# Half of the first layer's feed-forward, moved in 32 pieces into the first attention

## What is computed

```python
xn = _layernorm(x, axis=-1)
x = x + _L0_attn_ref(xn, Wq, Wk, Wv, Wo) + _L0_ffn_ref(xn, w_gate_up, w_down)
# _L0_attn_ref: 16 heads of 16, rotary embedding, causal softmax over 1024 tokens, output projection
# _L0_ffn_ref:
gate, up = jnp.split(jnp.einsum('bsh,oh->bso', xn, w_gate_up), 2, axis=-1)   # 1024 each
out = jnp.einsum('bsi,hi->bsh', jax.nn.silu(gate) * up, w_down)
```

## Time and profile before

| | us |
|---|---|
| three timed runs | 2784.49, 2780.20, 2782.88; median 2782.88 |
| profiled execution, its own time | 2753.76 |
| its span, first to last instruction | 2752.0 |
| Heads0, end (first matmul of Ffn at 448.13) | 448.1 |
| Ffn of layer 0, 448.1 to 617.1 | 169.0 |
| mean granted TensorE clock over the span | 0.979 |

### The profile page before, as it was taken

The page is one execution under the profiler, slowest core; times in us unless marked ns, Lnnn a source line. Parts: engine busy times, 40 slices in busy tenths (PEclk is TensorE's granted clock), DMA queues, the critical chain, the costliest instruction groups (busy, mean ns, idle before and its releaser), DMA issues.

```text
span 2752.0 us, 41999 instructions
## 1 busy us (share of the span) xinstructions
PE 2601.9 (95%) x16786; PEld 1644.6 (60%) x16786; DVE 1599.5 (58%) x3476; ACT 1064.0 (39%) x1954; POOL 926.3 (34%) x934
## 2 busy tenths in 40 slices
PE   7988988999999999999999998879999999979996
PEld 4445544664556565565665556646666666656896
DVE  6676672226575664756655232767778877754332
ACT  2534553114444534445445111533444444333222
POOL 3221210003232322322222001626666666654222
PEclk8999999999999999999999999989999999989998
DMA  6222211008000000000000200000000000036223
GB/s 191 63 62 63 62 47 62 0 4 148 1 1 1 1 1 1 1 1 1 1 16 1 106 0 31 1 13 17 17 15 16 15 15 17 14 130 190 62 72 134
DMA packets 57139, 109.54 MB, mean 40 GB/s; under 512 B 13793, under 2 KB 32481, under 8 KB 55793
## 3 DMA queue, kind: packets, MB, share of 16 engines
q1 hardware_dynamic: 53152, 96.47, 12.5%
q0 software_dynamic: 3792, 10.39, 1.0%
HBM read 71.16 MB, written 27.08 MB: 36 GB/s over the span
## 4 chain that ended last, share of the span: by engine, by line
PE 86%; DVE 8%; ACT 2%; issue 1%; DMA 1%; POOL 1%; SPq 1%; POOLq 0%; DVEq 0%; ACTq 0%
PE ps L1256 9%; PE ps L1238 8%; PE ps L1780 5%; PE ps L1247 5%; PE ps L1228 5%; PE ps L378 4%; PE ps L1265 4%; PE ps L360 4%; PE ps L365 4%; PE ps L1897 4%; PE ps L1826 4%; PE ps L2914 3%; PE ps L2938 3%; PE ps L697 2%; PE ps L721 2%; PE ps L737 2%
## 5 line engine op out<-in xcount | busy, mean ns | idle before, releaser
L1256 PE MATMUL ps<-back 128*128 128x512 f32 x576 | 292.0, 596 | 0.3 <-ACT back L1299 0.3
L1299 ACT ACTIVATE back<-ps 128x512 f32<-128x512 f32 x288 | 170.0, 597 | 266.3 <-PE ps L1247 264.7
L1294 ACT ACTIVATE back<-ps,front 128x128 f32<-128x128 f32 (+7 forms) x256 | 189.1, 739 | 71.6 <-DVE front L1345 69.5
L1388 POOL TENSOR_TENSOR back<-back 128x512 f32<-128x512 f32 x72 | 91.5, 1271 | 361.7 <-DVE back L1333 361.5
L1247 PEld LDWEIGHTS ps<-front,back 128*128 128x128 f32 x1152 | 140.8, 141 | 118.4 <-issue 95.0
L1398 POOL TENSOR_SCALAR back<-back,front 128x128 f32<-128x128 f32 (+5 forms) x192 | 143.1, 749 | 191.0 <-DVE front L1364 188.3
L809 ACT ACTIVATE back<-ps 128x1024 f32<-128x1024 f32 (+1 forms) x192 | 150.8, 811 | 127.9 <-PE ps L721 127.4
L1345 DVE TENSOR_REDUCE front<-ps 128x1 f32<-128x128 f32 (+7 forms) x256 | 194.0, 758 | 8.8
L1247 PE MATMUL ps<-front,back 128*128 128x128 f32 x1152 | 170.5, 273 | 3.3 <-DVE back L1370 3.3
L1338 DVE TENSOR_TENSOR ps<-ps,front 128x128 f32<-128x128 f32 x256 | 76.0, 297 | 166.1 <-PE ps L1238 166.1
L697 PE MATMUL ps<-rounded 128*128 128x512 f32 (+3 forms) x384 | 140.9, 410 | 12.6 <-DMA rounded<-kh 4.3
(11 more groups left out here) (320 smaller groups left out, 5562.8 us busy)
## 6 DMA issues: line engine op xcount, KB each, us to landing
whole<-l_w SPq DMA_DIRECT2D x32, 512.0 KB, 5.2
front<-back SPq DMA_DIRECT2D x128, 64.0 KB, 2.0
rounded<-qh SPq DMA_DIRECT2D x28, 256.0 KB
rounded<-kh SPq DMA_DIRECT2D x56, 128.0 KB
front<-xg SPq DMA_DIRECT2D x47, 129.0 KB
xg<-front SPq DMA_DIRECT2D x2, 3008.0 KB, 34.1
front<-l_win SPq DMA_DIRECT2D x1, 4640.0 KB, 17.7
front<-l_wgu SPq DMA_DIRECT2D x2, 2048.0 KB, 13.3
```

What stands on the lines that cost most here:

```text
L1256: e.matmul(PS[:, 7, :], self.V[:, j, G % 4 * 128:G % 4 * 128 + 128], self.turned(("turn", n, j)), start=(j == 0), stop=(j == qt)).then_inc ...
L1294: e.activation(self.P[n % 2][:, h, :nk], s[:, :nk], ACT.Exp, bias=st[:, 0, h:h + 1], scale=1.0, accum_out=st[:, 1, h:h + 1]).then_inc(A.se ...
L1299: e.activation(self.turned(step), self.bank(step), ACT.Copy).then_inc(A.sem, 1)
```

## The change

Of layer 0's feed-forward, tokens 0 to 1023 (8 groups t of 128 tokens) are computed within Heads0, the other 1024 stay in Ffn (`t0=2`).

- New steps `ff` 0 to 31 (four for each t): gate and up for 256 features and 128 tokens, 8 matmuls of 128 columns into one bank of the ring. ScalarE makes tanh(gate/2) into one buffer `th`; VectorE makes (th + 1) * gate, waits for itself, and makes that * 0.5 * up into one of four buffers `H`: silu(g) = g * (tanh(g/2) + 1) / 2.
- New steps `fd` 0 to 7: the down projection for 128 tokens, 8 matmuls of 256 columns, and one addition to x on VectorE.
- Places in time (`pieces`): two `ff` before the first unit's M transpose and two after it; then for each of units 1 to 14 one at three quarters of it and one just at the start of the next. `fd` 0 comes ahead of unit 1, `fd` 1 to 7 in the middle of units 3, 5, ..., 15.
- w_down is loaded in two halves after the first moves at the start, no longer at the end; `high` and `low` are half as long, so the two token halves of a projection share a buffer, and copies wait for the landing of the half before (`kept`, now one semaphore for each k, tt, x).
- Ffn runs tt = 2, 3 only; the norms of groups 0 and 1 are made behind ups 0 to 5 (`stats` and `rows` behind ups 0 and 3, `turn` behind 1 and 4, `out` behind 2 and 5). For t0 = 0 its order is as before.

The diff, cut to its core:

```diff
+        self.t0, self.ups, self.downs = t0, 8 * (4 - t0), 2 * (4 - t0)
...
-        for tt in range(5):
+        for tt in range(t0, 5):
             rest = [[("down", tt - 1, 0), ("down", tt - 1, 2), ("stats", tt - 1)], [("rows", tt - 1)],
-                    [("turn", tt - 1)], [("out", tt - 1)]] if tt else [[]] * 4
+                    [("turn", tt - 1)], [("out", tt - 1)]] if tt > t0 else [[]] * 4
             for f in range(8 if tt < 4 else 0):
                 self.order.add("up", tt, f)
+                if tt == t0 and f < 3 * t0:
+                    for kind in (("stats", "rows"), ("turn",), ("out",))[f % 3]:
+                        self.order.add(kind, f // 3)
...
-        self.low = [sb(WF0 + 4096 + 1024 * i, 1024) for i in range(2)]
+        self.low = [sb(WF0 + 4096 + 512 * i, 512) for i in range(2)]
+        self.Wd = [sb(WF0 + 5120, 4, 256), sb(WK0 + 17408, 4, 256)]
+        self.H = [sb(at, 256) for at in (EX0 + 512, EX0 + 768, WA0 + 12560, WF0 + 6144)]
+        self.th = sb(WK0 + 18944, 256)
...
-        self.high = [sbr(at + 16384 + 1024 * i, 1024) for i in range(2)]
+        self.high = [sbr(at + 16384 + 512 * i, 512) for i in range(2)]
...
+           "act": {"proj": 0.1, "v": -0.2, "s2": -0.15, "o": -0.05, "at": -0.2, "ff": -0.1},
...
-            elif step[0] in ("proj", "s1", "out", "ot"):
+            elif step[0] in ("proj", "s1", "out", "ot", "ff", "fd"):
...
+        if not pool:
+            for i, t in enumerate(self.pieces(begin, length)):
+                add(t, "ff", i)
+            if not act:
+                for i in range(8):
+                    add(begin[2 * i + 1] + (0.5 * length[2 * i + 1] if i else -0.25), "fd", i)
...
+    def pieces(self, begin, length):
+
+        at = [-0.07, -0.06, begin[0] - 0.04, begin[0] - 0.03]
+        for u in range(1, 15):
+            at += [begin[u] + 0.75 * length[u] + 0.14, begin[u + 1] + (0.12 if u in (7, 8) else 0.01)]
+        return at
...
+    def wait_kept(self, w, k, x, tt):
+
+        if tt > 0:
+            w.wait_ge(self.kept[k][0][x], 32)
+        elif k > 0:
+            w.wait_ge(self.kept[k - 1][1][x], 32)
...
+            elif kind == "ff":
+                t, f = step[1] // 4, 2 * (step[1] % 4)
+                w.wait_ge(self.ffn.arrived, self.ffn.total)
+                w.wait_ge(self.norm.out, t // 4 + 1)
+                o = self.take(w, step)
+                for side in range(2):
+                    for a in range(2):
+                        c = side * 1024 + (f + a) * 128
+                        at = side * 256 + a * 128
+                        for j in range(2):
+                            i = e.matmul(o[:, at:at + 128], self.Wgu[:, j, c:c + 128], XNT[:, j, t * 128:t * 128 + 128],
+                                         start=(j == 0), stop=(j == 1))
+                i.then_inc(P.sem, 1)
+            elif kind == "fd":
+                t = step[1]
+                w.wait_ge(self.wd_in, 32)
+                o = self.take(w, step)
+                w.wait_ge(self.results, self.dn["ff", 4 * t + 3])
+                for f in range(8):
+                    i = e.matmul(o[:, 0:256], self.H[f // 2][:, f % 2 * 128:f % 2 * 128 + 128],
+                                 self.Wd[f // 4][:, f % 4, :], start=(f == 0), stop=(f == 7))
+                i.then_inc(P.sem, 1)
...
-                e.activation(self.high[x][:, tt * 512:tt * 512 + 512], self.ra[x], ACT.Copy).then_inc(A.sem, 1)
+                self.wait_kept(w, k, x, tt)
+                e.activation(self.high[x], self.ra[x], ACT.Copy).then_inc(A.sem, 1)
...
+            elif kind == "ff":
+                w.wait_ge(self.products, self.pn[step])
+                if step[1] > 0:
+                    w.wait_ge(self.results, self.dn["ff", step[1] - 1])
+                e.activation(self.th, self.bank(step)[:, 0:256], ACT.Tanh, scale=0.5).then_inc(A.sem, 1)
...
+            elif kind == "ff":
+                n = step[1]
+                H = self.H[n % 4]
+                w.wait_ge(self.activations, self.an[step])
+                if n > 3:
+                    w.wait_ge(self.products, self.pn["fd", n // 4 - 1])
+                e.scalar_tensor_tensor(H, self.th, 1.0, self.bank(step)[:, 0:256], ALU.add,
+                                       ALU.mult).then_inc(self.half_done.sem, 1)
+                w.wait_ge(self.half_done, n + 1)
+                e.scalar_tensor_tensor(H, H, 0.5, self.bank(step)[:, 256:512], ALU.mult, ALU.mult).then_inc(D.sem, 1)
+            elif kind == "fd":
+                t = step[1]
+                w.wait_ge(self.products, self.pn[step])
+                before = ("out", 0, t // 2 * 2)
+                if self.dn[before] < self.dn[step]:
+                    w.wait_ge(D, self.dn[before])
+                e.tensor_tensor(X[:, t, :], X[:, t, :], self.bank(step)[:, 0:256], ALU.add).then_inc(D.sem, 1)
...
-                e.tensor_tensor(self.low[x][:, o], self.ra[x], self.high[x][:, o], ALU.subtract).then_inc(G.sem, 1)
+                self.wait_kept(w, k, x, tt)
+                e.tensor_tensor(self.low[x], self.ra[x], self.high[x], ALU.subtract).then_inc(G.sem, 1)
...
+        for i in range(2):
+            e.dma_start(self.Wd[i], self.net.ins["l0_wd"][:, 4 * i:4 * i + 4, :]).then_inc(self.wd_in.sem, 16)
...
-        w.wait_ge(self.results, self.dn["proj", 3, 1, 1, 0])
-        w.wait_ge(self.results, self.dn["proj", 3, 1, 1, 1])
-        e.dma_start(self.Wd, self.net.ins["l0_wd"]).then_inc(self.ffn.arrived.sem, 16)
...
-    f = Load(net, "w_ffn", [(Wgu, "l0_wgu")], 1)
-    h.plan(net, f, Norm(net, work=h.work, x=x), zeros)
+    f = Load(net, "w_ffn", [(Wgu, "l0_wgu")])
...
-    ffn = Ffn(net, Wgu, h.Wd, f, Norm(net, work=beside, inside=True, last=0))
+    ffn = Ffn(net, Wgu, [h.Wd[k // 4][:, k % 4, :] for k in range(8)], f, Norm(net, work=beside, inside=True, last=0), t0=2)
...
```

More of the change, by code:

```diff
@@ L907, in dve @@
                 w.wait_ge(self.products, self.pn[step])
+                for t in range(i, i + 2 if b == 0 else i):
+                    if self.dn["fd", t] < self.dn[step]:
+                        w.wait_ge(D, self.dn["fd", t])
                 e.tensor_tensor(x, x, self.bank(step).rearrange("p (a b) -> p a b", a=2), ALU.add).then_inc(D.sem, 1)
@@ L1191, in pe @@
         w.wait_ge(f.norm.out, 3)
-        w.wait_ge(f.x, 7)
+        w.wait_ge(f.x, f.downs - 1)
         for step in self.orders[0]:
@@ L3060, in stages @@
     q = Quantize(net)
-    ffn = Ffn(net, Wgu, Wd, f, Norm(net, work=beside, inside=True), side=q)
+    ffn = Ffn(net, Wgu, [Wd[:, k, :] for k in range(8)], f, Norm(net, work=beside, inside=True), side=q)
     m.late.after = [(q.high, 3), (ffn.u, 32)]
```

60 lines of the change are left out of this document (29 added, 31 removed).

## The result

The changed kernel takes 2792.69 us (median of 5 runs, 2791.01 to 2794.28); the kernel before takes 2782.88 us (5 runs, 2780.05 to 2784.49). The ratio is 1.0039 with a 95% interval of 1.0027 to 1.0052: **slower by 9.8 us**. The profiled execution took 2792.69 us, its span is 2790.9 us.

The account below looks back on a forecast made before the run. TensorE was taken to bound the feed-forward stage wholly, while the attention showed 49.0 us of TensorE idle time. Attention terms 6 + 13.4 + 37.5 + 25.5 - 2 = +80.4 us against -79.5 gave 2784 us, range 2761 to 2808.

Parts of the forecast that it names:

- Feed-forward stage: Layer 0's feed-forward: 82.6 us of ups and downs leave, 3.1 us of norm waits come; 79.5 us less (78 to 82.6).
- Start: First M transpose and first exponential: four pieces delay the exponential from 51.47 to about 60; +6 us (3 to 11).
- rival 4: Pieces on TensorE: bare weight loads of 192 ns make each 3.1 us instead of 1.79; 2825 us, chance 0.02.
- rival 3: ScalarE in the attention: tanh and exp share no table, so 28 pieces bring two loads each; 2838 us, chance 0.06.
- Ahead of the transposes: 14 turnovers: pieces of 25.1 us in all partly fill 12.05 us of TensorE waits for VectorE; +13.4 us.
- The clock term: Attention: pieces fill waits after which TensorE ran at 1.2 GHz; 2 us back in all (0 to 5).
- Behind the transposes: 14 turnovers: the tanh delays the first exponential, 2.9 us at eight, and VectorE binds six, 14.3 us; +37.5 us.
- Down pieces: Eight down projections within the attention, 2.6 to 3.4 us each, nearly their bare TensorE time; +25.5 us (16 to 28).
- Unit 9: Turnover into unit 9, one of six bound by VectorE: third s1 reduction about 7.3 us after the transpose; 2.4 us.
- The sum: Whole kernel: attention +80.4 us, feed-forward -79.5, net +0.9 us; 2784 us, no measurable change, chance 0.36.
- 1 (idle time filled, 2765): Attention: moved work fills part of TensorE's 49.0 us idle time, growth only 62 us; 2765 us, chance 0.33.
- 2 (the tanh ahead of the exponentials, 2802): ScalarE's order at 14 turnovers: the exponential's shift, 4.4 us each, is not made good; 2802 us, chance 0.23.

Follow-up runs that it names:

- e9: Changed kernel with only the two w_down loads moved on SP's queue, behind the moves of the second set of heads; ratio 1.0033 to the kernel before.
- e7: Changed kernel at half size: 16 pieces, all ahead of M transposes, 4 down pieces, 1536 tokens kept in the feed-forward stage; ratio 0.9991 to before.
- e1: Changed kernel without any ff or fd step in the attention, so that work is not computed; ratio 0.9713 to the kernel before.
- e3: Changed kernel without the 14 pieces ahead of an M transpose (ff 4, 6, ..., 30), not computed; ratio 0.9979 to the kernel before.
- e2: Changed kernel without the 14 pieces behind an M transpose (ff 5, 7, ..., 31), not computed; ratio 0.9905 to the kernel before.
- e5: Changed kernel with the tanh of the 14 pieces behind a transpose moved on ScalarE behind the new unit's first exponential; ratio 1.0012 to before.
- e8: Changed kernel with each matmul of the 14 pieces behind a transpose run twice into the same place; ratio 1.0128 to the kernel before.
- e4: Changed kernel without the eight fd steps (down projection and addition of the first 1024 tokens), not computed; ratio 0.9941 to the kernel before.
- e6: Changed kernel with only piece 18 moved, from directly ahead of the transpose at unit 8's end to earlier in that unit; ratio 1.0018 to before.
- e0: The changed kernel again, unaltered, on another chip with more runs; ratio 1.0029 to the kernel before.
- e10: e7 with the w_down loads later as in e9 and its first piece behind the first M transpose; ratio 0.9974 to before, median 2751.9 us.
- e11: Changed kernel in full size with the edits of e5, e6 and e9 together; ratio 1.0001 to the kernel before.

## Why the prediction was right in part

**Feed-forward stage.** Forecast -79.5, measured -79.7 us. The two waits for norm rows are there, 1.9 us in all, where I had taken 3.1 with the first up's table load. (By my own numbers, a chain of 5.9 us against an up of 3.44, the first wait would have been 2.5 and not 1.8.)

**Start.** +6 for the pieces and 2.6 for down piece 0 stood in the sum, 8.6; the transpose is at 49.92 instead of 46.22 and interval 0 is 4.9 us longer: 8.6. That it fits so well is partly luck, for the clock helped, and I had that as a term of its own: in interval 0 the granted clock is 0.96 for 0.81 before, and half speed costs 1.7 us for 6.5. The first exponential came at 60.9 (forecast about 60). The loads of w_down and the halved buffers were put at nothing, with up to 3 us if the cover goes: e9 confirms the cover, e7 shows it gone, and so does e1, where no pieces are left: its first wait for row transfers is 3.4 us longer than before, its attention 3.1.

**A piece.** 1.84 us for 1.79 from the earlier trace rows; rival 4 is out. The one table load moved to the first tanh (51.76), and no exponential of the attention has one: rival 3 is out. The trace agrees here with the Trainium skill, "ScalarE: Activation LUTs", section "Table sets: the hidden batching unit", which has tanh in the set of exp.

**Ahead of the transposes.** Forecast 13.4, measured 11.5 (e3), but by another account. I had 12 us of waits to fill, bare 1.79 us pieces and no clock in it; the runs show 3.8 us filled, 10.2 less lost to half speed, and one place, interval 9, that costs 5.5. The number was right by compensation. The clock term that I had apart (-2, 0 to 5) was 18.8 - 13.6 = 5.2 us over the start and attention, 4.8 of it in interval 0.

**Behind the transposes.** Forecast 37.5, measured 38.3 (e2). The size was right, the mechanism for eight of the turnovers was not. I had followed the tanh to the first exponential (3.2 us late, less 0.3 given back). e5 puts the exponential back to 3.3 us after its transpose and gains 3.6 us by it in four intervals; e8 doubles the matmuls and loses their full time. The cost is TensorE's 1.84 us plus waits for banks and exponentials of 0.8. My lower bound of 0.9 us for a turnover ("only what VectorE is given") was no bound: TensorE's own time was.

**Down pieces.** Forecast 25.5, measured 30.5 (e4). This term was mis-sized. I gave the pieces in four-block units and No. 7 less than their bare time or no more than it; none cost less than 3.4 us but No. 0, and three cost 5.1 with a low-clock stretch beside them.

**Unit 9.** The step that failed. The prediction's terms give 6.8 us to the interval (1.0 ahead, 2.4 behind, 3.4 for the down piece), as to its like (5 and 13); it took 11.8. I had written that three banks rotate and had reckoned with it for down pieces, but I did not walk the ring at the one turnover that has a projection right behind the transpose. e6 shows it: 3.0 us of wait. The other 1.7 us are a low-clock stretch behind the wait, which the changed kernel and e0 have and e5, e8 and e9, with the same wait, have not.

**The sum.** Attention +91.6 instead of +80.4; net +11.9 instead of +0.9 in the trace, +9.8 measured. By terms, the 11.2 us between 80.4 and 91.6 are: down pieces +5.0, what stays longer without any piece (e1) +3.1, the first four pieces 88.5 - 38.3 - 11.5 - 30.5 = 8.2 for 6, behind +0.8, ahead -1.9, and the -2 for the clock, which is already in these differences. By intervals, 5.0 of it is interval 9, in the terms of e3 and e4 both. (Each part was taken out by itself, so the first four pieces are only what is left over.) The time of 2792.7 us lies within the forecast's own 2775 to 2794, but the forecast's name for it, no measurable change, was wrong: two sums of 80 us with an error of a few per cent each can't tell 0 from 10.

**Rivals.** 1 (idle time filled, 2765): wrong, idle time rose from 49.0 to 55.7 us. 2 (the tanh ahead of the exponentials, 2802): the sign was right, and the mean turnover was (38.3 + 11.5) / 14 = 3.6 us, under the 4.0 from which I had let it decide; its mechanism is worth some 4 us (e5). What made the kernel slower was TensorE's own time at the turnovers, the down pieces and unit 9.

## What to carry to other kernels

Idle time that is spread in gaps of a microsecond along a chain is not room: at 14 places with 1.8 us pieces it swallowed 3.8 us, and made 10.8 us of new waits at 14 others. Price a moved piece at its full TensorE time unless the wait that it fills is named, compare that with what it costs where it is now, and keep only the places that win; here half of the pieces, 15 of 16 ahead of a transpose, together with later loads turned +8 us into -7. Before placing a step, walk the bank ring past it: with three banks in turn the third step behind it that takes one inherits its bank, and one such meeting cost 3.0 us of wait.

## What the hardware showed that I had not expected

Code that the change doesn't touch took up to 27 us more from chip to chip, more than the whole effect. From 2500 to 2600 us TensorE is busy for 80.0 us at a granted clock of 0.83 in the changed kernel's profile; the same kernel in e0, on another chip:

```profile
2500.00:2600.00 100.00, 96.70 (x506) 75.48 (x507) 41.47 (x94) 30.40 (x61) 36.19 (x39) 0.98 0.46 146
```

96.7 us and 0.98 there; 97.8 and 1.00 in before and e10. (The same window doesn't hold quite the same work in each, as the executions are up to 44 us apart by then.) In the changed kernel waits of several microseconds come first, two of them with no releaser that the profile shows, and then the longest low-clock stretch of its layer 3, 30.7 us:

```profile
2515.02 0.69 PE L2854 MATMUL ps<-front 128*128 128x128 f32 x2 [5.39 <-issue]
2520.49 2.07 PE L2860 MATMUL ps<-front 128*128 128x256 f32 x4 [3.93 <-issue]
```

Five profiles have this, the changed kernel's and those of e5 to e8, whose chips gave before a median of 2782.9 or 2782.3 us: in them TensorE is idle for 38 to 43 us between 2300 and 2700 us. The eight on the chips where before has 2757.4 or 2757.1 (e0 to e4, e9 to e11) don't have it, whatever the kernel: 20 to 22 us. The profiled execution of before (2753.76 us, 26 below the fastest of its timed runs) looks like these eight. So from the start of layer 1 to the end the changed kernel's profile took 27 us longer than before's and that of e0 only 8. It goes with the chip; what makes the waits stays open.

A wait alone doesn't decide whether the clock falls. The projection behind a wait of 3.02 us ran for 5.40 us in unit 9 of the changed kernel (granted clock 0.50 from 336 to 338 us, the level of 1.2 GHz), and for 3.70 us, at 2.4 GHz, behind that of e10 in unit 1 (86.27, shown above), behind the very same wait in e9 (335.13, shown above) and in e8:

```profile
346.18 3.70 PE L700 MATMUL ps<-front 128*128 128x512 f32 x8 [3.01 <-DVE front L907]
```

Nor does the amount of work decide what half speed costs: 18.8 us before, 23.9 in e1, 8.5 in e4, 13.6 in the changed kernel and 11.9 in e0, the same kernel again.
